# Cross attention: softmax sums inverted in SBUF, turned maxima placed by DMA, values and sums issued apart

## The chip, the cores and the metric

One core of one Trainium2 chip. The metric is the device time of one execution in microseconds. The kernel is a whole decoder layer; the change touches one of its stages.

## The reference

A decoder layer on x (2 batches, 2048 positions, 512 features, float32) does self attention, then cross attention, then a feed-forward part with experts. The change lies in the cross attention: 16 heads of 32 features, 154 keys per batch.

```python
scores = jnp.einsum('bhtd,bhsd->bhts', q, k) * scale
scores = jnp.where(causal_mask[None, None], neg_inf, scores)
scores = jnp.where(key_padding_mask[:, None, None, :], neg_inf, scores)
attn = jax.nn.softmax(scores, axis=-1)
out = jnp.einsum('bhts,bhsd->bhtd', attn, v)
```

Queries beyond position 153 see all keys, so of each batch's four blocks of 512 queries only the first has a causal mask.

## The kernel before

`cross_attention` (from line 1186) works in 32 units: eight blocks of 512 queries (two batches of four) times four groups of four heads. Units 0 to 3 and 16 to 19 are causal. For a unit there are these parts, spread over the units around it:

- `scores(u, s)`, eight slots of two 128-query tiles of one head, queries on partitions, 154 keys along the row (L1325). q and k are stacks of 96 rows (high and low parts), with rows for maxima and padding beneath. Causal units add the mask with a bf16 matmul against an identity (L1328). Slots go to three banks of `ps_s`.
- DVE takes the negated maximum of each slot (`slot_max`, L1404), splits the 16 columns of a unit in a high and a low part (`max_rows` of DVE, L1414 and L1416) in `max_parts`.
- `turn_max(u)` on TensorE (L1338) multiplies `max_parts`, 128 columns of which 8 hold values, with an identity, so that the maxima lie along rows; ACT copies two rows for each of four heads into rows 96 and 97 of `q_stack` (L1460).
- `transposed_scores(u, t)`, eight tiles (four heads, two halves of 77 keys) with keys on partitions, the maxima subtracted by the two added rows (L1350; causal units add a mask, L1353); ACT takes the exponential of each (L1469). These tiles and the turn share the three banks of `ps_st`.
- `weighted_values(u)` (L1364) and `totals(u)`, the sums of the probabilities over keys (L1373), each 16 matmul instructions in the trace, into one bank, `ps_pv` and `ps_d`. ACT copies `ps_pv` to `attn_raw` (L1476).
- DVE inverts the sums in place in PSUM, in four pieces of 128 columns (`invert`, L1422), multiplies (`normalize`, L1429), and SP stores the result (L1290).

The order on each engine is written out by hand. TensorE in unit u issues for t = 0 to 7 a transposed tile of u and a scores slot of u + 2 (called a tile below, together); ahead of t = 3 stand the turn of u + 1, the weighted values and the totals of u - 1. `totals(u)` waits until `normalize(u - 1)` has read `ps_d`. DVE puts the reciprocals between the slots, two pieces behind slots 3 and 4 and two behind slots 0 and 1 of the next unit, and the normalization behind slot 2. ACT follows TensorE's order. `transposed_scores(u, 0)` waits for ACT's copies of the maxima.

SP loads in order: q of unit 0, both stacks of k of batch 0 (that for scores and that for transposed scores), identities, masks, q of unit 1, v, q of units 2 and 3, k of batch 1, and the weights of the next stage (`ahead`, 2.5 MB), which GpSimd splits in two parts (L71, L74). No load among these waits for computed data. Then, per unit, it stores unit u - 2 and loads q of unit u + 4 into the buffer that unit u has left. TensorE starts once all constants and masks are there (`consts_loaded`, 80).

## Time and profile before

| what | us |
|---|---|
| median of three runs | 3406.66 |
| lowest and highest run | 3405.03, 3454.39 |
| the profiled execution, its time | 3420.66 |
| its span, first to last instruction | 3418.9 |
| TensorE busy in the span | 3061.5 |
| DVE busy | 2181.1 |
| ACT busy | 1672.3 |
| GpSimd busy | 1718.2 |
| mean granted clock of TensorE, as a share of 2.4 GHz | 0.925 |
| the cross attention, from its first memset to the last store's landing | about 2433 to 2862 |

The profiled execution is one of its own; its time stands between the runs, and its span is 1.8 us less than its time. Times in the trace count from the span's start. A granted clock of 1.00 is 2.4 GHz and of 0.50 is 1.2 GHz; values between are means over a stretch that has both. Instructions are merged in the timelines when they are alike and adjacent; their ends are modelled for matmuls, so the start of the next is the better mark.

### The profile page before, as it was taken

What the parts mean: (1) busy time and instruction counts of PE and PEld (TensorE: products, weight loads), DVE (VectorE), ACT (ScalarE), POOL (GpSimd) and SP (SyncE); (2) the same over time, 40 slices, a digit from 0 to 9 for tenths busy, and PEclk for the clock granted to TensorE, in tenths of its full rate; (3) what the DMA queues carried; (4) which work ended last, traced back from release to release, by engine and by line L of the source; (5) the groups of instructions that cost most, each with busy time, mean ns of one, the idle gap of its engine ahead of it and who ended that gap; (6) DMA issues with size and microseconds to landing.
All of it is one profiled execution on the core that took longest, in us unless ns stands there. A gap on an engine that the chain in (4) does not pass through costs nothing. (4 is left out here: it accounts for less than half of the span.)

```text
span 3418.9 us, 41782 instructions
## 1 busy us (share of the span) xinstructions
PE 3061.5 (90%) x15214; PEld 1750.2 (51%) x15214; DVE 2181.1 (64%) x3987; ACT 1672.3 (49%) x3029; POOL 1718.2 (50%) x694
## 2 busy tenths in 40 slices
PE   7997999999999999999999997696489986989488
PEld 6875444444444444444444442575345542777433
DVE  4334788788888888888888882463265574566322
ACT  2221466666666666666666665221076672222111
POOL 0001388787888878788888878000210001333255
PEclk9998799999999999999999999798696796999679
DMA  4545545646456464465554443597632232333621
GB/s 173 182 174 171 114 93 107 135 94 151 86 109 135 104 143 99 102 133 108 129 113 96 90 93 65 184 265 169 178 113 86 83 94 106 123 123 116 215 72 35
DMA packets 171357, 424.22 MB, mean 124 GB/s; under 512 B 19105, under 2 KB 40514, under 8 KB 151172
## 3 DMA queue, kind: packets, MB, share of 16 engines
q1 hardware_dynamic: 147038, 276.97, 27.9%
q0 software_dynamic: 24128, 144.75, 20.1%
q8 instruction: 115, 1.88, 0.2%
q14 instruction: 76, 0.62, 0.1%
HBM read 170.20 MB, written 124.58 MB: 86 GB/s over the span
## 5 line engine op out<-in xcount | busy, mean ns | idle before, releaser
L654 DVE TENSOR_REDUCE part_max<-ps_s 128x1 f32<-128x512 f32 x2048 | 1270.3, 679 | 313.2 <-PE ps_s L555 313.2
L751 ACT ACTIVATE probs<-ps_st 128x512 f32<-128x512 f32 x2048 | 1086.4, 600 | 549.3 <-PE ps_st L574 533.9
L513 POOL TENSOR_TENSOR added<-added,probs 128x2048 f32<-128x2048 f32 x256 | 1181.9, 4617 | 93.0 <-ACT probs L751 66.9
L555 PE MATMUL ps_s<-k_stack,q_stack 96*128 96x512 f32 x2048 | 842.1, 427 | 28.3 <-POOL max_parts L503 20.6
L574 PE MATMUL ps_st<-q_stack,k_stack 98*128 98x512 f32 x2048 | 857.7, 424 | 6.6 <-ACT probs L751 5.4
L574 PEld LDWEIGHTS ps_st<-q_stack,k_stack 98*128 98x128 f32 x2048 | 386.9, 190 | 505.6 <-ACT probs L751 362.1
L585 PE MATMUL ps_pv<-probs,v_sb 128*32 128x512 f32 x4096 | 547.2, 606 | 0.0
L555 PEld LDWEIGHTS ps_s<-k_stack,q_stack 96*128 96x128 f32 x2048 | 396.0, 193 | 213.9 <-DVE part_max L654 142.8
L521 POOL DMA_DIRECT2D probs<-probs x128 | 112.7, 880 | 232.7 <-PE ps_pv L585 219.1
L1404 DVE TENSOR_REDUCE xneg_max<-xps_s 128x2 f32<-128x308 f32 x256 | 110.6, 448 | 130.8 <-PE xps_s L1325 82.2
L1654 POOL MEMSET e_bias_rows<- 128x1024 f32 x1 | 1.0, 952 | 354.3 <-POOLq L46 354.3
L1325 PE MATMUL xps_s<-xks_stack,xq_stack 99*128 99x154 f32 (+1 forms) x512 | 130.7, 336 | 49.1 <-DVE xident_r L1436 38.7
L513 POOL TENSOR_TENSOR added<-probs 128x2048 f32<-128x2048 f32 x32 | 146.3, 4570 | 48.7 <-ACT probs L751 48.7
L679 DVE RECIPROCAL ps_d<-ps_d 128x128 f32<-128x128 f32 x128 | 121.0, 949 | 63.2 <-PE ps_d L600 63.2
L585 PEld LDWEIGHTS ps_pv<-probs,v_sb 128*32 128x32 f32 x4096 | 80.8, 108 | 151.8 <-ACT probs L751 122.8
L1325 PEld LDWEIGHTS xps_s<-xks_stack,xq_stack 99*128 99x128 f32 (+1 forms) x512 | 116.4, 234 | 76.8 <-issue 43.4
L1469 ACT ACTIVATE xprobs<-xps_st,xpad_bias 77x512 f32<-77x512 f32 x192 | 119.3, 683 | 69.5 <-PE xps_st L1350 67.1
L1422 DVE RECIPROCAL xps_d<-xps_d 128x128 f32<-128x128 f32 x128 | 120.5, 948 | 19.4 <-PE xps_d L1373 19.4
L1350 PE MATMUL xps_st<-xq_stack,xkt_stack 98*77 98x512 f32 x256 | 122.9, 487 | 1.0 <-ACT xq_stack L1460 0.8
L229 DVE TENSOR_TENSOR qk_l_out<-ps_g,qk_h_out 128x512 fp32r<-128x512 f32 x64 | 43.3, 688 | 125.9 <-ACT qk_h_out L266 125.9
L187 POOL TENSOR_TENSOR rstd<-var_eps,minus_half 128x4 f32<-128x4 f32 x8 | 8.1, 1014 | 224.4 <-DVE var_eps L207 224.4
L1460 ACT ACTIVATE xq_stack<-xps_st 2x512 fp32r<-2x512 f32 x128 | 75.2, 588 | 70.7 <-PE xps_st L1338 69.1
(268 smaller groups left out, 3633.1 us busy)
## 6 DMA issues: line engine op xcount, KB each, us to landing
probs<-probs POOLq DMA_DIRECT2D x128, 1024.0 KB, 7.0
xq_stack<-q_parts SPq DMA_DIRECT2D x64, 384.0 KB, 4.4
q_stack<-q_hi SPq DMA_DIRECT2D x64, 256.0 KB, 6.1
k_stack<-k_hi SPq DMA_DIRECT2D x64, 256.0 KB, 9.0
q_parts<-q_h_out SPq DMA_DIRECT2D x64, 256.0 KB, 4.9
x_in<-in_x_rows SPq DMA_DIRECT2D x8, 1024.0 KB, 7.1
q_hi<-qk_h_out SPq DMA_DIRECT2D x8, 1024.0 KB, 4.3
q_lo<-qk_l_out SPq DMA_DIRECT2D x8, 1024.0 KB, 6.3
```

Of the source, the lines that this page charges most:

```text
L513: pool.tensor_tensor(added[:, w % 2], left, probs[:, k % RING], ALU.add).then_inc(added_up, 1)
L521: pool.dma_start(probs[:, k % RING].rearrange("p j q -> p (j q)"), probs[:, (k - 1) % RING].rearrange("p j q -> p (j q)"), accum_op=ALU.ad ...
L555: pe.matmul(ps_s[:, place % BANKS], q_stack[0:ROWS, w % 4, j, t * P:(t + 1) * P], k_stack[0:ROWS, w // BPB, j, n * BLK:(n + 1) * BLK], sta ...
L574: pe.matmul(ps_st[:, n % BANKS], k_stack[:, w // BPB, j, k * P:(k + 1) * P], q_stack[:, w % 4, j], start=True, stop=True).then_inc(item_do ...
L585: mm = pe.matmul(ps_pv[j * HD:(j + 1) * HD], v_sb[:, w // BPB, k, j * HD:(j + 1) * HD], probs[:, k % RING, j], start=(k == 0), stop=(k == ...
L654: dve.tensor_reduce(part_max[:, s:s + 1], ps_s[:, (w * SLOTS + s) % BANKS], AX.X, ALU.max)\
L679: dve.reciprocal(ps_d[:, cols], ps_d[:, cols]).then_inc(inverted, 1)
L751: act.activation(probs[:, k % RING, j], ps_st[:, n % BANKS], ACT.Exp, scale=SCALE).then_inc(item_used, 1)
L1325: mm = pe.matmul(out, q_stack[0:top, u % BUFS, j, t * P:(t + 1) * P], ks_stack[0:top, batch(u), u % QUADS * HEADS + j], start=True, stop=n ...
L1350: mm = pe.matmul(out, kt_stack[:, batch(u), u % QUADS * HEADS + j, h * KH:(h + 1) * KH], q_stack[0:TOP, u % BUFS, j], start=True, stop=not ...
L1422: dve.reciprocal(ps_d[:, cols], ps_d[:, cols]).then_inc(inverted, 1)
L1469: act.activation(probs[:, u % 2, t % 2, t // 2], ps_st[0:KH, n % BANKS], ACT.Exp, scale=SCALE, **bias)\
```

## The change

1. `totals(u)` is copied by ACT from PSUM to a new tile `sums` in SBUF (`sums_out`); DVE inverts it there in two pieces of 256 columns and the normalization reads it there. `totals(u)` now waits for the copy of u - 1, not for its normalization.
2. `max_parts` has 8 columns per tile, so that the turn writes 8 rows. ACT copies them in one instruction to a new tile `row_parts`, and SP places two rows for each of the four heads in `q_stack` with four DMAs (`rows_into_place`); `transposed_scores(u, 0)` waits for these.
3. The turn stands ahead of t = 2, the weighted values ahead of t = 4, the totals behind t = 7. DVE's first piece stands ahead of slot 4, its second and the normalization at the unit's end, both for unit u - 2. The store is a unit later.
4. The loads are reordered: q of unit 1 ahead of the transposed k, masks last; the rows of unit 0 ahead of v and the q of units 2 and 3, and those of unit 1 ahead of the k of batch 1 and the weights ahead. Waits are split, so that scores start without the transposed k and masks.

```diff
-        BEFORE_TURN = 3
+        BEFORE_TURN = 2
+        BEFORE_VALUES = 4
+        PIECES = 2
...
-        max_parts = sb("xmax_parts", [P, TPB, P], F32R)
+        max_parts = sb("xmax_parts", [P, TPB, 2 * HEADS], F32R)
+        row_parts = sb("xrow_parts", [2 * HEADS, 2, BLK], F32R)
...
+        sums = sb("xsums", [P, 2, BLK])
...
-        k_loaded = [sem(f"xk_loaded{b}") for b in range(B)]
+        ks_loaded, kt_loaded = ([sem(f"x{n}_loaded{b}") for b in range(B)] for n in ("ks", "kt"))
...
+        rows_loaded = [sem(f"xrows_loaded{s}") for s in range(2)]
...
-                def load_k(b):
-                    sp.dma_start(ks_stack[0:ROWS, b].bitcast(F32), xk_parts[:, b]).then_inc(k_loaded[b], 16)
+                def load_scores_k(b):
+                    sp.dma_start(ks_stack[0:ROWS, b].bitcast(F32), xk_parts[:, b]).then_inc(ks_loaded[b], 16)
                     sp.dma_start(ks_stack[TOP:TOP + 1, b].bitcast(F32),
-                                 pad_row[b].unsqueeze(0).unsqueeze(0).to_broadcast([1, H, SC])).then_inc(k_loaded[b], 16)
-                    sp.dma_start(kt_stack[0:ROWS, b].bitcast(F32), xk_parts[:, b]).then_inc(k_loaded[b], 16)
+                                 pad_row[b].unsqueeze(0).unsqueeze(0).to_broadcast([1, H, SC])).then_inc(ks_loaded[b], 16)
+
+                def load_transposed_k(b):
+                    sp.dma_start(kt_stack[0:ROWS, b].bitcast(F32), xk_parts[:, b]).then_inc(kt_loaded[b], 16)
...
                 sp.wait_ge(ones_set, 2)
                 load_q(0)
-                load_k(0)
+                load_scores_k(0)
                 sp.dma_start(ident[:], eye).then_inc(consts_loaded, 16)
                 sp.dma_start(ident_bf[:], eye_bf).then_inc(consts_loaded, 16)
                 sp.dma_start(mq[:].rearrange("p b t k -> p (b t k)"), mask_q).then_inc(consts_loaded, 16)
...
                 sp.wait_ge(ones_set, 4)
-                sp.dma_start(mk[0:KH].rearrange("p b h k -> p (b h k)"), mask_k).then_inc(consts_loaded, 16)
-                sp.dma_start(pad_bias[:], pad_scaled).then_inc(consts_loaded, 16)
                 load_q(1)
+                load_transposed_k(0)
+                sp.dma_start(mk[0:KH].rearrange("p b h k -> p (b h k)"), mask_k).then_inc(masks_loaded, 16)
+                sp.dma_start(pad_bias[:], pad_scaled).then_inc(masks_loaded, 16)
+
+                def rows_into_place(u):
+
+                    sp.wait_ge(item_used, turn_item(u) + 1)
+                    for j in range(HEADS):
+                        sp.dma_start(q_stack[ROWS:TOP, u % BUFS, j].bitcast(F32),
+                                     row_parts[2 * j:2 * j + 2, u % 2].bitcast(F32)).then_inc(rows_loaded[u % 2], 16)
+
+                rows_into_place(0)
                 sp.dma_start(v_sb[:], xv_rows).then_inc(v_loaded, 16)
                 load_q(2)
                 load_q(3)
-                load_k(1)
-                ahead.load(sp)
-                for u in range(UNITS + 2):
-                    if exists(u - 2):
-                        n, g = (u - 2) // QUADS, (u - 2) % QUADS
-                        sp.wait_ge(normalized, u - 1)
-                        sp.dma_start(out_units[n // BPB, n % BPB, g], attn_out[:, u % 2]).then_inc(out_stored[u % 2], 16)
+                for u in range(UNITS + 3):
+                    if exists(u + 1):
+                        rows_into_place(u + 1)
+                    if u == 0:
+                        load_scores_k(1)
+                        load_transposed_k(1)
+                        ahead.load(sp)
+                    if exists(u - 3):
+                        n, g = (u - 3) // QUADS, (u - 3) % QUADS
+                        sp.wait_ge(normalized, u - 2)
+                        sp.dma_start(out_units[n // BPB, n % BPB, g], attn_out[:, (u - 3) % 2])\
+                          .then_inc(out_stored[(u - 3) % 2], 16)
                     if exists(u + BUFS):
                         sp.wait_ge(item_done, item(u, TILES - 1) + 1)
                         load_q(u + BUFS)
...
-                                                   (max_parts[:].bitcast(F32), 0.0), (ones[:], 1.0))):
+                                                   (ones[:], 1.0))):
...
-                        pe.wait_ge(k_loaded[batch(u)], 48)
+                        pe.wait_ge(ks_loaded[batch(u)], 32)
...
-                        mm = pe.matmul(ps_st[:, n % BANKS, t * P:(t + 1) * P], max_parts[:, t], ident_r[:],
+                        mm = pe.matmul(ps_st[0:2 * HEADS, n % BANKS, t * P:(t + 1) * P], max_parts[:, t], ident_r[:],
...
                     if t == 0:
-                        pe.wait_ge(item_used, turn_item(u) + 1)
+                        pe.wait_ge(rows_loaded[u % 2], 64 * (u // 2 + 1))
+                        pe.wait_ge(kt_loaded[batch(u)], 16)
+                        pe.wait_ge(masks_loaded, 32)
...
                 def totals(u):
                     if u:
-                        pe.wait_ge(normalized, u)
+                        pe.wait_ge(sums_done, u)
...
-                pe.wait_ge(ones_set, 6)
-                pe.wait_ge(consts_loaded, 80)
+                pe.wait_ge(ones_set, 5)
+                pe.wait_ge(consts_loaded, 48)
...
                     scores(1, s)
                 for u in range(UNITS + 1):
                     for t in range(TILES):
-                        if t == BEFORE_TURN:
-                            if exists(u + 1):
-                                turn_max(u + 1)
-                            if exists(u - 1):
-                                weighted_values(u - 1)
-                                totals(u - 1)
+                        if t == BEFORE_TURN and exists(u + 1):
+                            turn_max(u + 1)
+                        if t == BEFORE_VALUES and exists(u - 1):
+                            weighted_values(u - 1)
                         if exists(u):
                             transposed_scores(u, t)
                         if exists(u + 2):
                             scores(u + 2, t)
+                    if exists(u - 1):
+                        totals(u - 1)
...
                 def invert(u, q):
-                    cols = slice(q * P, (q + 1) * P)
-                    dve.wait_ge(dens_done, u + 1)
-                    dve.reciprocal(ps_d[:, cols], ps_d[:, cols]).then_inc(inverted, 1)
+                    cols = slice(q * BLK // PIECES, (q + 1) * BLK // PIECES)
+                    dve.wait_ge(sums_done, u + 1)
+                    dve.reciprocal(sums[:, u % 2, cols], sums[:, u % 2, cols]).then_inc(inverted, 1)
 
                 def normalize(u):
                     dve.wait_ge(raw_done, u + 1)
                     if u >= 2:
                         dve.wait_ge(out_stored[u % 2], 16 * (u // 2))
-                    dve.wait_ge(inverted, TPB * (u + 1))
-                    dve.tensor_tensor(attn_out[:, u % 2], ps_d[:], attn_raw[:, u % 2], ALU.mult).then_inc(normalized, 1)
+                    dve.wait_ge(inverted, PIECES * (u + 1))
+                    dve.tensor_tensor(attn_out[:, u % 2], sums[:, u % 2], attn_raw[:, u % 2], ALU.mult).then_inc(normalized, 1)
...
                 for u in range(UNITS + 2):
                     for s in range(SLOTS):
+                        if s == BEFORE_VALUES and exists(u - 2):
+                            invert(u - 2, 0)
                         if exists(u + 2):
                             slot_max(u + 2, s)
-                        if exists(u - 2) and s < 2:
-                            invert(u - 2, s + 2)
-                        if exists(u - 2) and s == 2:
-                            normalize(u - 2)
-                        if exists(u - 1) and 3 <= s < 5:
-                            invert(u - 1, s - 3)
                     if exists(u + 2):
                         max_rows(u + 2)
+                    if exists(u - 2):
+                        invert(u - 2, 1)
+                        normalize(u - 2)
...
                 def max_rows(u):
                     n = turn_item(u)
                     act.wait_ge(item_done, n + 1)
-                    for j in range(HEADS):
-                        mm = act.activation(q_stack[ROWS:TOP, u % BUFS, j], ps_st[j * HD:j * HD + 2, n % BANKS], ACT.Copy)
-                    mm.then_inc(item_used, 1)
+                    if u >= 2:
+                        act.wait_ge(rows_loaded[u % 2], 64 * (u // 2))
+                    act.activation(row_parts[:, u % 2], ps_st[0:2 * HEADS, n % BANKS], ACT.Copy).then_inc(item_used, 1)
...
-                act.wait_ge(ones_set, 6)
-                act.wait_ge(consts_loaded, 80)
+                def sums_out(u):
+                    if u >= 2:
+                        act.wait_ge(normalized, u - 1)
+                    act.wait_ge(dens_done, u + 1)
+                    act.activation(sums[:, u % 2], ps_d[:], ACT.Copy).then_inc(sums_done, 1)
+
                 max_rows(0)
+                act.wait_ge(masks_loaded, 32)
                 for u in range(UNITS + 1):
                     for t in range(TILES):
-                        if t == BEFORE_TURN:
-                            if exists(u + 1):
-                                max_rows(u + 1)
-                            if exists(u - 1):
-                                raw_out(u - 1)
+                        if t == BEFORE_TURN and exists(u + 1):
+                            max_rows(u + 1)
+                        if t == BEFORE_VALUES and exists(u - 1):
+                            raw_out(u - 1)
                         if exists(u):
                             exponentials(u, t)
+                    if exists(u - 1):
+                        sums_out(u - 1)
```

## Rows read from the trace of the kernel before

**Rows 1.** Windows of the cross attention: busy us (instructions) by engine, granted clock, DMA share, GB/s

```profile
2496.00:2514.00 18.00, 16.10 (x71) 8.14 (x71) 10.59 (x16) 7.63 (x14) 11.77 (x5) 0.62 0.21 60
2514.00:2589.00 75.00, 64.77 (x462) 34.91 (x464) 55.76 (x114) 59.31 (x100) 0.00 (x0) 1.00 0.37 109
2589.00:2692.00 103.00, 103.00 (x448) 55.87 (x444) 48.84 (x97) 53.24 (x84) 0.00 (x0) 0.50 0.22 64
2692.00:2822.00 130.00, 114.55 (x819) 62.06 (x817) 94.46 (x193) 99.97 (x169) 0.00 (x0) 1.00 0.35 100
2822.00:2862.00 40.00, 30.57 (x118) 8.36 (x118) 16.82 (x24) 14.53 (x25) 0.00 (x0) 0.53 0.07 27
...
2684.60:2691.20 6.60, 6.60 (x30) 4.48 (x27) 3.43 (x6) 2.38 (x4) 0.00 (x0) 0.50 0.00 0
```

**Rows 2.** Grouped instructions of nine units at clock 1.00, 2726.68 to 2816.88 us

```profile
L1469 ACT ACTIVATE xprobs<-xps_st,xpad_bias 77x512 f32<-77x512 f32 x72 | 43.4, 682 | 19.6 <-PE xps_st L1350 19.6
L1422 DVE RECIPROCAL xps_d<-xps_d 128x128 f32<-128x128 f32 x36 | 34.3, 952 | 0.0
...
L1460 ACT ACTIVATE xq_stack<-xps_st 2x512 fp32r<-2x512 f32 x37 | 21.7, 588 | 0.5
...
L1429 DVE TENSOR_TENSOR xattn_out<-xps_d,xattn_raw 128x512 f32<-128x512 f32 x9 | 6.1, 673 | 0.0
```

**Rows 3.** Waits in the same stretch: total us, times, longest us

```profile
DVE xneg_max L1404 <- PE xps_s L1325: 23.3, 9, 2.6
```

**Rows 4.** Timeline of one unit at clock 1.00: start, us, engine, line, instruction

```profile
2744.10 0.66 PE L1338 MATMUL xps_st<-xident_r,xmax_parts 128*128 128x128 f32 x4
...
2744.69 1.92 PE L1364 MATMUL xps_pv<-xprobs,xv_sb 77*32 77x512 f32 x16
...
2747.46 1.92 PE L1373 MATMUL xps_d<-xprobs,xones 77*32 77x512 f32 x16 [0.85 <-DVE xattn_out L1429]
...
2749.32 0.46 PE L1350 MATMUL xps_st<-xq_stack,xkt_stack 98*77 98x512 f32 x1
...
2749.80 0.40 PE L1350 MATMUL xps_st<-xq_stack,xkt_stack 98*77 98x512 f32 x1
...
2750.22 0.40 PE L1350 MATMUL xps_st<-xq_stack,xkt_stack 98*77 98x512 f32 x1
```

**Rows 5.** Timeline of TensorE around 2612 us, at clock 0.50

```profile
2612.01 0.63 PE L1350 MATMUL xps_st<-xq_stack,xkt_stack 98*77 98x512 f32 x1
...
2612.77 1.03 PE L1338 MATMUL xps_st<-xident_r,xmax_parts 128*128 128x128 f32 x4
2613.74 3.64 PE L1364 MATMUL xps_pv<-xprobs,xv_sb 77*32 77x512 f32 x16
2617.15 3.64 PE L1373 MATMUL xps_d<-xprobs,xones 77*32 77x512 f32 x16
2620.72 0.71 PE L1350 MATMUL xps_st<-xq_stack,xkt_stack 98*77 98x512 f32 x1
```

**Rows 6.** Timeline of TensorE: last tile before unit 2, its first, unit 30's first

```profile
2495.19 0.44 PE L1350 MATMUL xps_st<-xq_stack,xkt_stack 98*77 98x512 f32 x1
...
2496.00 0.43 PE L1350 MATMUL xps_st<-xq_stack,xkt_stack 98*77 98x512 f32 x1
...
2822.19 1.29 PE L1350 MATMUL xps_st<-xq_stack,xkt_stack 98*77 98x512 f32 x3
```

**Rows 7.** First load; window of loads; landings of pad rows (L1267), then of output stores (L1290)

```profile
2444.04 0.79 SPq L1262 DMA_DIRECT2D xq_stack<-q_parts  x2
...
2460.00:2470.00 10.00, 7.16 (x39) 7.03 (x39) 4.51 (x12) 0.00 (x0) 0.00 (x0) 0.50 1.03 255
...
DMA to landing us min/median/max: 9.1/15.9/22.6
...
DMA to landing us min/median/max: 2.3/2.3/4.6
```

**Rows 8.** Timeline near 2497 us: DVE's cast of the maxima

```profile
2496.75 1.36 DVE L1414 CAST xmax_parts<-xneg_max 128x16 fp32r<-128x16 f32 x1
```

More of the change, by code:

```diff
@@ L1225, in cross_attention @@
                                            for n, (_, high, _) in enumerate(weights_ahead)])
-        k_loaded = [sem(f"xk_loaded{b}") for b in range(B)]
+        ks_loaded, kt_loaded = ([sem(f"x{n}_loaded{b}") for b in range(B)] for n in ("ks", "kt"))
         v_loaded = sem("xv_loaded")
         q_loaded = [sem(f"xq_loaded{s}") for s in range(BUFS)]
-        consts_loaded, ones_set, ident_ready = sem("xconsts_loaded"), sem("xones_set"), sem("xident_ready")
+        consts_loaded, masks_loaded = sem("xconsts_loaded"), sem("xmasks_loaded")
+        ones_set, ident_ready = sem("xones_set"), sem("xident_ready")
         scores_done, max_done = sem("xscores_done"), sem("xmax_done")
@@ L1232, in cross_attention @@
         item_done, item_used = sem("xitem_done"), sem("xitem_used")
+        rows_loaded = [sem(f"xrows_loaded{s}") for s in range(2)]
         pv_done, dens_done = sem("xpv_done"), sem("xdens_done")
-        raw_done, inverted, normalized = sem("xraw_done"), sem("xinverted"), sem("xnormalized")
+        raw_done, sums_done = sem("xraw_done"), sem("xsums_done")
+        inverted, normalized = sem("xinverted"), sem("xnormalized")
         out_stored = [sem(f"xout_stored{s}") for s in range(2)]
@@ L1304, in _ @@
                     pool.memset(tile, value).then_inc(ones_set, 1)
-                pool.wait_ge(ones_set, 6)
+                pool.wait_ge(ones_set, 5)
                 for step in range(ahead.STEPS):
@@ L1433, in slots @@
                         slot_max(u, s)
-                dve.wait_ge(consts_loaded, 80)
+                dve.wait_ge(consts_loaded, 48)
                 dve.tensor_copy(ident_r[:], ident[:]).then_inc(ident_ready, 1)
-                dve.wait_ge(ones_set, 6)
+                dve.wait_ge(ones_set, 5)
                 for u in range(2):
```

## The prediction

> **What bounds the kernel now.** I read the stage's windows first. The reader is to see one stage at two speeds: from 2589 to 2692 us TensorE is busy for all of the 103 us and its granted clock is 0.50, the 1.2 GHz level; from 2692 to 2822 us it is at 1.00, 2.4 GHz, and busy for only 114.55 of 130 us [rows 1]. At the low level TensorE itself is the bound. At the high level something else is, and the grouped instructions of nine units there say what: 72 exponentials are nine times eight, so a unit takes 90.2 / 9 = 10.02 us, in which ACT holds four copies of two rows at 588 ns each beside eight exponentials, and DVE four reciprocals at 952 ns beside eight maxima [rows 2]. The waits show the loop that sets the 10.02: DVE is idle 2.6 us per unit for scores [rows 3]. The timeline tells why: weighted values start at 2744.69, the sums could follow at once, but wait 0.85 us for the normalization, because that reads the sums in PSUM; then the sums, 1.86 us to the next transposed scores, stand between the normalization and DVE's next scores [rows 4]. So DVE works, then TensorE works, and each waits for the other.
>
> At 1.2 GHz a tile (transposed scores and scores) takes 2612.77 - 2612.01 = 0.76 us, the turn 0.97, the weighted values 3.41, the sums 3.57: 8 x 0.76 + 7.95 = 14.0 us, with nothing idle [rows 5].
>
> **The change part by part.**
>
> *Sums copied to SBUF.* It adds one ACT copy of 128x512, which no row of mine shows by itself; bounds are the 588 ns of a 2x512 copy and the 682 ns of an exponential with bias [rows 2]. I take 0.6. It removes the wait of the sums for the normalization (0.85 us, and the 2.6 us of DVE behind it), as PSUM is free again after that copy.
>
> *Reciprocals, two of 256 columns for four of 128.* Bounds: 0.95 us (width costs nothing) and 1.90 us (twice the row) for one [rows 2]. I take 1.8, near the upper end, as an iterated division should go by column. DVE's work was 94.46 us in 130, which is 7.3 us in a unit of 10.02 [rows 1]; it becomes about 7.2.
>
> *Turned maxima in eight rows.* Three of four ACT copies go, 3 x 0.588 = 1.76 us of ACT a unit, 0.6 comes back for the sums: ACT, a near bound, is left with some 6.9 us. The turn itself writes 8 rows in place of 128; its 0.59 us (2744.10 to 2744.69) lies between 0.3 and 0.6, I take 0.5 [rows 4]. Its matmul needs no more DVE work than now.
>
> *Four row DMAs per unit on SP's queue,* behind the turn's copy. The next transposed scores now wait for them. One output store lands in 2.3 us [rows 7], issued in some 0.35; four issues and a landing are 1.4 + 2.3 = 3.7 us after the copy. The turn is at tile 2, six tiles, the weighted values and the sums before the next unit: 6 x 0.42 at least + 3.6 = 6.1 us of cover less 1.5 for copy and handoff, so 4.6 against 3.7: hidden by about a microsecond. Bounds: 0, and, if each took the 9.1 us that a small transfer took behind large ones, 4.5 us a unit [rows 7]. In the steady state nothing large is ahead of them: the q loads are issued at a unit's end, some 3.5 us earlier. I take 0. SP's queue is in order: the rows are issued before the output store, both before the q load of the same turn, which waits last; nothing else of SP's is urgent.
>
> *Weighted values at tile 4, sums at the unit's end.* No work changes. DVE's first reciprocal (1.8) now lies beside the weighted values (1.8), its second, with the normalization (0.67), beside the sums (1.86), and three score banks bridge the rest. By hand for a unit at 2.4 GHz: TensorE 8 x 0.43 + 0.5 + 1.8 + 1.85 = 7.6; DVE 7.2 plus about 0.5 of handoffs. I take 7.75 (low 7.3, ACT's and DVE's sum; high 9.0, if half of the old handoff is left).
>
> *The beginning,* an estimate from one rate. Scores can start earlier, as they no longer wait for the transposed k and masks. But SP now sits at unit 0's turn before it issues v and q of units 2 and 3, and at unit 1's before the second k and the weights ahead, 4.3 MB. Before, these were issued without such waits. SP's first load goes out at 2444.04, and the DMA moves 255 GB/s [rows 7]. What the first scores need is 2.2 MB, so they begin near 2456; eight slots and the turn later, near 2465, ACT releases the rows of unit 0; after them v and one q, 1.4 MB, land at about 2474, where unit 0 starts (before at 2475.4). Its turn comes some 5 us later, so the 4.3 MB and the next q, 5.2 MB or 20 us, flow from about 2483.5. The rows of unit 2 are issued behind them. The row of the small pad transfer shows what that does: 9.6 KB took 9.1 and 22.6 us to land behind large loads [rows 7]. So unit 2 starts near 2503.7, not at 2496.00 [rows 6]: plus 7.7 us, and TensorE is idle for about 9 us ahead of it. Bounds: 0 and 12.
>
> *Sum.* From unit 2 to unit 30 the kernel took 2822.19 - 2496.00 = 326.2 us for 28 units [rows 6]. After: 20 units without causal work x 7.75 = 155; 14 and 15 (causal scores only), tile between 0.42 and 0.81, taken 0.55: 8.7 each; 16 and 17, 0.81 a tile [rows 6]: 8 x 0.81 + 4.2 = 10.7 each; 18, 19 and 3 (causal transposed scores only), tile 0.63: 9.2 each; unit 2, partly at 1.2 GHz: 14. In all 155 + 17.4 + 21.4 + 27.6 + 14 = 235.4: minus 90.8. The start adds 7.7. The tail of 40 us at clock 0.53 [rows 1] loses about 2.5 us of idleness. Net minus 85.6 on the profiled execution's 3420.7: 3335. Its own time is 14 us above the median of the runs, 3406.7, and the low stretch (103 us) may be shorter in those, of which little remains here; other stages may account for some of it. I take 2 off: 3333 us.
>
> **The clock, and a page.** Of the 90.8 us, 103 x (1 - 10.02 / 14.0) = 29 come from the low stretch alone, which is assumed at 2.4 GHz. Before TensorE's clock fell there, it had run turn, weighted values and the wait for DVE as in every unit [rows 4]; before it rose again it had been busy for the whole 6.6 us up to 2691.2, in tiles with causal mask matmuls [rows 1]. Tiles without them, eight between sums and turn, did not bring it back. The new order leaves no pause at 2.4 GHz, so I expect no fall; but after the pause at unit 2 it needs a rise, and its runs of tiles are cut in two.
>
> The Trainium skill, TensorE: Matmul & The Clock Gate, section "Why this matters for your kernels", says that TensorE that is kept continuously busy gets the full clock. The trace disagrees: 103 us without idleness at 0.50 [rows 1]. By the page the clock would be back within unit 2 and the result some 5 us lower; by the row it may not rise for ten units, which is the first rival below.
>
> A second page speaks against the move to SBUF: SBUF — State Buffer, section "SBUF: two separate sides", says that a VectorE instruction with two SBUF inputs and a GpSimd instruction block one another. The normalization becomes such an instruction. The trace agrees in kind: a cast of 16 columns took 1.36 us while GpSimd split weights [rows 8], and GpSimd is busy 11.77 of those 18 us [rows 1]. It has no work later in this stage, so by the page it is at most a few microseconds, once, beside unit 2.
>
> **The rivals.**
>
> *The clock stays low after the start (chance 0.18; the other side).* The mechanism: TensorE's pause before unit 2 drops it to 1.2 GHz; units 2 and 3 have causal mask matmuls in their tiles but now in two runs of four with weighted values or sums between, and if they don't lift it, ten units without causal work don't either, as those of the low stretch did not. Price: 10 x (14.0 - 7.75) = 62, units 2 and 3 +11, 14 and 15 +15, half of 16 +5: 93 us, so 3426, slower than 3406.7. It decides at unit 3's end. For it: the 103 us. Against: a pause at 2498 us also lowered the clock (0.62 over 2496 to 2514) and causal units brought it back by 2514 [rows 1].
>
> *Rows come late (0.10).* If four landings follow one another or queue behind the q load, each unit waits 1 to 1.5 us for them: 24 x 1.2 = 29: 3362. For: the 22.6 us row. Against: the 2.3 us row.
>
> *The start costs nothing (0.10).* If the loads drain sooner, or small transfers pass, unit 2 starts at 2496 and the clock holds: 3333 - 8 (the start) - 7 (the low part of units 2 and 3) = 3318.
>
> *Forecast (0.62),* own range 3305 to 3360: 7.4 to 8.6 a unit is -7 to +17 on 20 units, the start -5 to +5.
>
> **How the numbers follow.** The range 3302 to 3428 takes in the forecast, the cheap start, the late rows and half of the low clock. About 2% (68 us) is what a measurement of this kernel tells from no change, so faster means below 3338.5. Of the forecast 0.6 lies there (0.37), of the cheap start all (0.10), of the late rows little (0.01): faster 0.48, same 0.47, slower 0.05 (the clock low also past unit 20, another 60 us or more).
>
> **What would show it.** Units at 2.4 GHz 7.5 to 8 us apart; 256-column reciprocals near 1.8 us and starting beside weighted values and sums; no wait of sums for the normalization; DVE's wait for scores under 0.5 us a unit; row DMAs landing in 2 to 3 us with transposed scores not waiting for them after unit 2; a pause of 5 to 12 us before unit 2. A unit above 9 us at clock 1.00 refutes the handoff argument; a stretch of clock 0.50 from unit 2 to unit 16 is the first rival.

## The result, and the profile after

The changed kernel takes 3331.23 us (median of 3329.57, 3330.77, 3331.69 and 3414.33), against 3426.44 for the kernel before in the same rounds (3405.03 to 3454.39): ratio 0.9731, interval 0.967 to 0.9791. The forecast was 3333. The ratio leaves out the fourth run, which had a mean granted clock of 0.917 where the profiled one had 0.946; it lies near the 3426 at which the first rival was priced, and is told of below.

The windows of the cross attention, in the columns of [rows 1], cut where the clock changed:

```profile
2481.00:2498.00 17.00, 14.41 (x114) 8.67 (x112) 7.00 (x18) 9.34 (x16) 0.00 (x0) 1.00 0.89 255
2498.00:2508.30 10.30, 4.81 (x19) 3.35 (x19) 1.36 (x3) 2.36 (x4) 6.75 (x3) 0.50 0.67 177
2508.30:2530.00 21.70, 20.36 (x151) 10.56 (x150) 19.15 (x29) 13.04 (x23) 9.67 (x4) 1.00 0.32 88
2530.00:2600.00 70.00, 69.09 (x512) 37.55 (x508) 65.18 (x112) 52.72 (x93) 0.00 (x0) 1.00 0.45 128
2600.00:2700.00 100.00, 99.43 (x761) 54.84 (x758) 87.07 (x144) 68.54 (x122) 0.00 (x0) 1.00 0.41 120
2700.00:2760.00 60.00, 57.45 (x416) 29.28 (x419) 53.38 (x84) 45.86 (x82) 0.00 (x0) 1.00 0.35 100
```

One dip to 0.50, then 1.00 to the end. The 103 us stretch of [rows 1] is gone, and TensorE is busy for 99% where it was busy for 88%. The grouped instructions of 2530 to 2600 us answer to [rows 2]:

```profile
L1494 ACT ACTIVATE xprobs<-xps_st,xpad_bias 77x512 f32<-77x512 f32 x68 | 41.4, 676 | 0.0
L1448 DVE RECIPROCAL xsums<-xsums 128x256 f32<-128x256 f32 x18 | 31.4, 1743 | 0.0
...
L1455 DVE TENSOR_TENSOR xattn_out<-xsums,xattn_raw 128x512 f32<-128x512 f32 x8 | 5.5, 692 | 1.1
L1501 ACT ACTIVATE xattn_raw<-xps_pv 128x512 f32<-128x512 f32 x9 | 5.4, 598 | 9.7 <-PE xps_pv L1390 9.7
```

68 exponentials in 70 us are 8.5 units of 8.2 us; ACT's copies of the weighted values, one a unit, stand 8.27 us apart, where they stood 10.02. The reciprocal of 256 columns takes 1743 ns. The waits of the same stretch:

```profile
PEld xps_st L1376 <- ACT xprobs L1494: 10.0, 17, 0.8
ACT xattn_raw L1501 <- PE xps_pv L1390: 9.7, 9, 1.1
ACT xsums L1507 <- PE xps_d L1399: 7.7, 8, 1.0
...
DVE xneg_max L1430 <- PE xps_s L1349: 2.2, 9, 0.3
```

DVE's wait for scores was 2.6 us a unit in [rows 3] and is 0.3. No wait of the sums for the normalization is left in this stretch. What is late now is in the first line: twice a unit the weight load of a transposed tile waits for an exponential to free its PSUM bank. TensorE's timeline of one unit shows what that costs:

```profile
2558.96 0.46 PE L1376 MATMUL xps_st<-xq_stack,xkt_stack 98*77 98x512 f32 x1
...
2559.44 0.40 PE L1376 MATMUL xps_st<-xq_stack,xkt_stack 98*77 98x512 f32 x1
...
2559.86 0.41 PE L1362 MATMUL xps_st<-xident_r,xmax_parts 128*8 128x128 f32 x4
2560.38 0.46 PE L1376 MATMUL xps_st<-xq_stack,xkt_stack 98*77 98x512 f32 x1
...
2560.95 0.46 PE L1376 MATMUL xps_st<-xq_stack,xkt_stack 98*77 98x512 f32 x1
...
2561.53 1.92 PE L1390 MATMUL xps_pv<-xprobs,xv_sb 77*32 77x512 f32 x16
2563.38 0.46 PE L1376 MATMUL xps_st<-xq_stack,xkt_stack 98*77 98x512 f32 x1
...
2565.37 1.07 PE L1399 MATMUL xps_d<-xprobs,xones 77*32 77x512 f32 x8
```

From start to start: tiles 0.48 and 0.42, turn 0.52, tiles 0.57 and 0.58, values 1.85, and the other four tiles 1.99 (2563.38 to 2565.37); the sums, 2557.10 to 2558.96, took 1.86. Together 8.27 us: in each group of four tiles the last two follow one another at 0.5 to 0.6 us, nearer to ACT's 0.68 for an exponential than to TensorE's 0.43.

The beginning, TensorE and SyncE before unit 2:

```profile
2491.11 2.43 SPq L1296 DMA_DIRECT2D xq_stack<-xrow_parts  x4
...
2503.49 0.71 PE L1376 MATMUL xps_st<-xq_stack,xkt_stack 98*77 98x512 f32 x1 [8.07 <-DMA xq_stack<-xrow_parts]
```

The first line is SyncE issuing the four row DMAs of unit 2, behind 4.3 MB of loads; TensorE waits 8.07 us for them, the only wait of the stage for row DMAs. Each of the 128 row DMAs took 0.56 to 0.70 us to issue.

### The profile page after: what moved, and what is told of

The parts are those of the page before. It is cut to its first block and busy times, and to the rows that moved or that the text cites. A ratio compares the mean times of both kernels' runs of the same rounds, so it can differ in the third digit from the quotient of the medians.

```text
span 3327.8 us, 41873 instructions
## 1 busy us (share of the span) xinstructions
PE 2984.6 (90%) x15214; PEld 1715.5 (52%) x15214; DVE 2191.5 (66%) x3923; ACT 1620.7 (49%) x2965; POOL 1718.3 (52%) x693
## 5 line engine op out<-in xcount | busy, mean ns | idle before, releaser
L1349 PE MATMUL xps_s<-xks_stack,xq_stack 99*128 99x154 f32 (+1 forms) x512 | 113.5, 300 | 42.0 <-DVE xident_r L1462 32.5
L1349 PEld LDWEIGHTS xps_s<-xks_stack,xq_stack 99*128 99x128 f32 (+1 forms) x512 | 104.4, 205 | 59.8 <-issue 43.9
L1376 PE MATMUL xps_st<-xq_stack,xkt_stack 98*77 98x512 f32 x256 | 111.4, 440 | 12.7 <-DMA xq_stack<-xrow_parts 8.1
L1448 DVE RECIPROCAL xsums<-xsums 128x256 f32<-128x256 f32 x64 | 111.0, 1740 | 6.1 <-ACT xsums L1507 6.1
L908 POOL TENSOR_TENSOR c_rstd<-c_var_eps,c_minus_half 128x4 f32<-128x4 f32 x8 | 8.1, 1009 | 195.5 <-DVE c_var_eps L941 195.5
```

Source lines behind the costliest of these rows:

```text
L1349: mm = pe.matmul(out, q_stack[0:top, u % BUFS, j, t * P:(t + 1) * P], ks_stack[0:top, batch(u), u % QUADS * HEADS + j], start=True, stop=n ...
L1376: mm = pe.matmul(out, kt_stack[:, batch(u), u % QUADS * HEADS + j, h * KH:(h + 1) * KH], q_stack[0:TOP, u % BUFS, j], start=True, stop=not ...
```

## The experiments

The "unit" below is the distance of ACT's copies of the weighted values in units without causal work.

**Sums left in PSUM** (`e1_psum`).

```diff
-                        pe.wait_ge(sums_done, u)
+                        pe.wait_ge(normalized, u)
...
-                    dve.reciprocal(sums[:, u % 2, cols], sums[:, u % 2, cols]).then_inc(inverted, 1)
+                    dve.reciprocal(ps_d[:, cols], ps_d[:, cols]).then_inc(inverted, 1)
...
-                    if exists(u - 1):
-                        sums_out(u - 1)
```

The normalization reads `ps_d` again.

> The changed kernel with the sums left in PSUM: no ACT copy of them, both 256-column reciprocals and the normalization work on PSUM, and the sums of a unit wait for the normalization of the one before. Order, row DMAs and loads as changed. Theory (the handoff over PSUM is what cost 2 us a unit): the sums at a unit's end wait for a reciprocal and the normalization, about 2.5 us, and a unit without causal work goes from 8.27 back to 10.0 to 10.8 us at clock 1.00; total 3375 to 3430, the upper half if the clock falls as well. Rival (the new order alone, with fewer copies on ACT, gives the gain): under 9 us a unit and under 3345.

Measured 3596.5 us (3592.9 to 3601), ratio 1.0497 (1.0418 to 1.0577). Its waits of 2600 to 2700 us, and the end of one unit:

```profile
DVE xneg_max L1430 <- PE xps_s L1349: 51.0, 47, 4.7
...
PEld xps_d L1399 <- DVE xattn_out L1455: 18.6, 5, 3.7
```

```profile
2612.20 3.64 PE L1399 MATMUL xps_d<-xprobs,xones 77*32 77x512 f32 x16 [3.51 <-DVE xattn_out L1455]
...
2616.86 0.48 DVE L1430 TENSOR_REDUCE xneg_max<-xps_s 128x2 f32<-128x308 f32 x1 [4.72 <-PE xps_s L1349]
```

The wait returns, as expected, but at 3.51 us a unit, and the clock is at 0.50 for the whole of that window. A unit takes 17.7 us: the 14.2 of 1.2 GHz plus the wait. The time is 166 us above the top of what was expected, because I had priced the units at clock 1.00. The clock fell at 2543 us, behind the first such wait at 1.00 (3.48 us, up to 2542.26), and was 0.50 from 2550 to 2760. So the copy to SBUF is what makes the rest of the new order work, and the first such wait at 1.00 was followed by the loss of the clock as well. That the later waits kept the clock down is not shown: `e6_b_sums` and `e3_late` have long stretches at 0.50 without any idle.

**That copy alone, in the kernel before** (`e6_b_sums`), with its four pieces:

```diff
-                        pe.wait_ge(normalized, u)
+                        pe.wait_ge(sums_done, u)
...
                                 raw_out(u - 1)
+                                sums_out(u - 1)
```

> The kernel before with one part of the change: ACT copies the sums to SBUF, right behind the weighted values' copy, and DVE inverts them there in four pieces. Theory (the copy pays only with the new order and the freed ACT): the 0.85 us wait of TensorE goes, but ACT has 8.7 us of work in a unit and the copy stands ahead of five exponentials: 9.3 to 9.9 us a unit, total 3385 to 3420. Rival: 8.3 us and under 3350.

Measured 3432.81 us (3404 to 3453, ten runs), ratio 1.004 (0.9998 to 1.0081). The unit at clock 1.00 is 8.96 us, a little quicker than expected; the total is not, by these windows:

```profile
2532.00:2678.00 146.00, 146.00 (x630) 79.06 (x630) 74.17 (x151) 88.25 (x140) 0.00 (x0) 0.50 0.25 73
2700.00:2760.00 60.00, 57.82 (x420) 32.09 (x419) 47.37 (x97) 54.15 (x93) 0.00 (x0) 1.00 0.40 120
```

The 1.06 us a unit were won and given back by a longer low stretch (146 us, where [rows 1] had 103) and a second one from 2764. The copy is needed, and not enough. No long idle stood ahead of either fall. Ahead of the first one:

```profile
2500.00:2532.00 32.00, 30.82 (x220) 18.29 (x223) 26.57 (x56) 29.01 (x50) 3.10 (x2) 1.00 0.41 124
...
2530.10 0.45 PE L1327 MATMUL xps_s<-xks_stack,xq_stack 99*128 99x154 f32 x2 [0.51 <-DVE xneg_max L1406]
```

The longest wait of TensorE there is this one of 0.51 us, which comes once in most units of this kernel, and the same wait stands at 2762.20 ahead of the second fall. Why the clock fell at these units, and in the kernel before at 2589 us, is open.

**Turn, values and sums together ahead of tile 3, sums in SBUF** (`e5_together`).

```diff
-        BEFORE_TURN = 2
-        BEFORE_VALUES = 4
+        BEFORE_TURN = 3
+        BEFORE_VALUES = 3
...
                             weighted_values(u - 1)
+                            totals(u - 1)
...
                             raw_out(u - 1)
+                            sums_out(u - 1)
```

The two calls at the unit's end are gone.

> The changed kernel with turn, weighted values and sums together ahead of tile 3, as before (raw and sums copies by ACT there too; DVE's first reciprocal ahead of slot 3). Sums in SBUF, row DMAs and loads as changed. Theory (the two stretches of 1.8 us must be apart, since three score banks hold DVE's work for one of them only): DVE waits some 1.5 us for scores, 9.3 to 10.2 us a unit at clock 1.00, total 3352 to 3400. Rival (the copy to SBUF alone gives the gain): 8.1 to 8.5 us a unit, 3331.

Measured 3333.8 us (3329.8 to 3341.9), ratio 0.9763 (0.9701 to 0.9824), unit 8.28, and from 2570 to 2640 us TensorE busy for 69.76 of 70 at clock 1.00. The theory is refuted and the rival holds: the order of values and sums gives nothing that this can measure. With the copy and without four row copies, both orders run alike.

**Rows by four ACT copies in place of four DMAs** (`e2_rows_act`); the turn writes 128 rows again and `rows_into_place` is gone.

```diff
-                    act.activation(row_parts[:, u % 2], ps_st[0:2 * HEADS, n % BANKS], ACT.Copy).then_inc(item_used, 1)
+                    for j in range(HEADS):
+                        mm = act.activation(q_stack[ROWS:TOP, u % BUFS, j], ps_st[j * HD:j * HD + 2, n % BANKS], ACT.Copy)
+                    mm.then_inc(item_used, 1)
```

> The changed kernel with the maxima turned into 128 rows and copied by ACT in four pieces straight into the q stack, as before; no row DMAs, so SP's loads wait for nothing at the start. Theory: ACT gets 1.75 us more in a unit, which its waits of 1.9 us in 8.27 do not all cover: 8.6 to 9.2 us a unit, 20 units give plus 7 to 19; the pause of 8 us ahead of unit 2 is gone (minus 8 to 15); total 3322 to 3342. Rival (the row DMAs are what carries the gain): 10 us a unit, 3360 or more. Rival (the row DMAs cost what they save): 8.27 a unit and 3318.

Four runs: 3352.2, 3353.9, 3425.9 and 3429.8 us, the last two at mean clock 0.916 and 0.915 against 0.94. In the profiled run (3353.9) the unit is 9.17 us at clock 1.00, so the DMAs are worth 0.9 us a unit in the steady state. The pause before unit 2 is absent: the values' copies around it stand 14.70 us apart (2490.43 and 2505.13), 20.40 in the changed kernel, so the DMAs cost 5.7 us there. The unit is as expected; the total is 10 to 12 us above the top of what was expected in the two runs at 0.94, and over 80 in the others. Those two show that a run some 75 us longer at a lower mean clock comes without the 8 us pause too; they have no profile.

**The burst of loads moved from unit 0 to unit 4** (`e3_late`).

```diff
-                    if u == 0:
+                    if u == 4:
                         load_scores_k(1)
                         load_transposed_k(1)
                         ahead.load(sp)
```

> The changed kernel with the k of batch 1 and the weights ahead loaded at unit 4 and not at unit 0. Theory (these 4.3 MB in front of the rows of unit 2 make the pause of 8 us and the drop of the clock): no pause ahead of unit 2, units unchanged at 8.27 us; total 3314 to 3322, and no run near 3414 in three rounds, as nothing lowers the clock before ten units that cannot lift it. Rival (the pause is hidden, or the rows come late by themselves): 3328 to 3334; rival for the one run at 3414 (its source lies elsewhere): such a run comes here too.

Measured 3392.16 us (3390.4 to 3400.2, ten runs), ratio 0.9938 (0.9911 to 0.9965): 61 us slower than the changed kernel. Its timeline at unit 6 and a window behind it:

```profile
2546.27 0.71 PE L1376 MATMUL xps_st<-xq_stack,xkt_stack 98*77 98x512 f32 x1 [10.29 <-DMA xq_stack<-xrow_parts]
```

```profile
2550.00:2698.00 148.00, 148.00 (x640) 75.22 (x640) 82.27 (x129) 70.49 (x110) 8.07 (x4) 0.50 0.25 73
```

The pause went with the burst, which shows its cause. The expected 3314 to 3322 was missed by 70 us: I had not seen that the burst would hold the rows of unit 6 in place of those of unit 2. There no unit with causal tiles follows soon, and the clock stays at 0.50 with TensorE busy for all of these 148 us. This is the first rival's mechanism. The profiled run shows it; all ten runs have a mean clock of 0.921 to 0.924, so it came in each.

**ACT's sums copy behind two exponentials of the next unit** (`e4_sums_later`).

```diff
+                        if t == BEFORE_TURN and exists(u - 2):
+                            sums_out(u - 2)
...
-                    if exists(u - 1):
-                        sums_out(u - 1)
```

> The changed kernel with ACT's copy of the sums moved behind two exponentials and the copy of the maxima of the next unit. Theory (8.27 and not 7.75 us, because the copy of the sums stands ahead of the exponential that frees the bank for the tile behind the turn): 7.8 to 8.0 us a unit, total 3321 to 3328. Rival (DVE's two reciprocals of 1.74 us set 8.27): 8.2 to 8.3 us and no change.

Measured 3328.12 us (3326.8 to 3336.5), ratio 0.9715 (0.9643 to 0.9788); the unit 8.18 us, 0.09 less and not the 7.8 to 8.0 of the theory. TensorE has no idle time left (60.00 of 60 us busy). I read DVE, idle for 1.3 us in 60 by its waits, as the bound. That reading was tested next. The start of this run shows something else:

```profile
2508.00:2528.00 20.00, 19.79 (x79) 10.60 (x80) 9.01 (x15) 6.95 (x13) 13.82 (x5) 0.50 0.15 43
```

The pause before unit 2 is nearly that of the changed kernel (7.29 us for 8.07), but TensorE, busy again from 2506.25, stays at 0.50 for 22 us, into the middle of unit 3, the last causal one of the first batch; in the changed kernel it was 5 us.

**1.6 us of DVE work a unit taken away** (`e9_short`, `e10_short_sums`): the second reciprocal of a unit inverts 16 columns and leaves 240 uninverted, in the changed kernel and in the last one.

```diff
-                    cols = slice(q * BLK // PIECES, (q + 1) * BLK // PIECES)
+                    cols = slice(q * BLK // PIECES, (q + 1) * BLK // PIECES) if q == 0 else slice(BLK // 2, BLK // 2 + 16)
```

> The changed kernel with the second reciprocal of a unit cut from 256 columns to 16 (half of the sums then stays uninverted, which the output shows): about 1.6 us of VectorE work less a unit, nothing else changed. A unit took 8.27 us, with VectorE 7.7 us of it busy. Theory A (the ring of TensorE and ScalarE through the turned exponentials, with ScalarE's copy of the sums ahead of the next unit's first exponential, sets the 8.27 us, and VectorE only follows): a unit stays at 8.1 to 8.27 us, and TensorE stays busy all but 0.1 us of it. Theory B (VectorE's 7.7 us with its handoffs set it): a unit of 7.5 to 7.7 us, TensorE's own work being 7.4 to 7.6 at clock 1.00, and over the stage some 14 us less.

> The same cut with ScalarE's copy of the sums moved behind the next unit's second exponential, where a unit took 8.18 us and VectorE was idle for only 0.16 us of it. Theory (in that kernel VectorE sets the unit, by 8.0 us of busy time and handoffs): with 1.6 us of its work gone TensorE's own work is left, a unit of 7.5 to 7.8 us, 12 to 20 us less over the stage than the 8.18 us unit makes. Rival (TensorE sets 8.18 as well, its busy time being counted too short by the model of matmul ends): a unit stays at 8.1 to 8.2 us and the time within 3 us of 3328.

One run each: 3332.4 and 3328.6 us, units of 8.27 and 8.14. Windows 2540 to 2600 us of the first, and its DVE wait:

```profile
2540.00:2600.00 60.00, 59.21 (x442) 31.83 (x431) 47.19 (x96) 44.85 (x81) 0.00 (x0) 1.00 0.45 135
```

```profile
DVE xneg_max L1430 <- PE xps_s L1349: 9.9, 22, 0.5
```

DVE's work fell from 56.00 us in the changed kernel to 47.19 in this window and the unit did not move: DVE only waits more. Theory A holds in the changed kernel, and in the other my DVE theory falls, the rival holding at 8.14 against 8.18. What is left to set the unit is TensorE and ACT's exponentials through the PSUM banks. Which of those two, and whether a fourth bank would give the rest, was not tried.

**The burst spread: k loads at units 2 and 3, the next stage's three weights one at a time at units 15 to 17** (`e7_spread`), and the same with the later sums copy (`e8_spread_sums`).

```diff
-                    if u == 0:
+                    if u == 2:
                         load_scores_k(1)
+                    if u == 3:
                         load_transposed_k(1)
-                        ahead.load(sp)
+                    if 15 <= u < 15 + len(ahead.weights):
+                        source, raw, _, _ = ahead.weights[u - 15]
+                        sp.dma_start(raw, source).then_inc(ahead.loaded, 16)
```

> The changed kernel with the k of batch 1 loaded at units 2 and 3 and the three weights ahead at units 15, 16 and 17, one load of about 1 MB at a time behind the rows. Theory (a burst of 4.3 MB ahead of the rows makes the pause, and a pause lets the clock fall, for ten units where they have no causal work): no pause of over 2 us behind unit 0, clock 1.00 from about 2487 us to the end of the stage, 8.27 us a unit; total 3314 to 3323, and none of the runs of five rounds above 3350. Rival (the one run at 3414 has a source elsewhere): again a run some 80 us above the others. Rival (any single load of 1 MB delays the rows past 8.27 us): pauses of 1 to 3 us in units 3, 4 and 16 to 18.

> The spread loads together with ACT's copy of the sums behind the copy of the maxima. Theory: both gains add, 8.18 us a unit as measured with the copy moved alone: 2 us below the run with spread loads, 3311 to 3321, and the interval of its ratio to the kernel before below 0.975. Rival: GpSimd's work at units 17 to 19 meets DVE's and costs back 2 us or more.

Measured 3329.59 (3326.3 to 3337.6; ratio 0.9749) and 3325.74 us (3321.9 to 3330.0 and one of 3399.51; ratio 0.9735, 0.9683 to 0.9788). Both are above what was expected (3314 to 3323 and 3311 to 3321). The pause before unit 2 is gone, the clock is 1.00 from 2482 us; but GpSimd now splits the weights beside busy units, all three in one stretch, since it waits for the last of them (`pool.wait_ge(self.loaded, 16 * len(self.weights))`). The second kernel there:

```profile
2636.36 4.64 POOL L74 TENSOR_TENSOR xwo_w_l<-xahead_raw,xwo_w_h 128x2048 fp32r<-128x2048 f32 x1
2640.84 2.00 POOL L71 CAST xwo_w_h<-xahead_raw 128x2048 fp32r<-128x2048 f32 x1
...
2643.82 0.71 PE L1352 MATMUL xps_s<-xks_stack,xq_stack 99*128 99x154 f32 x2 [5.51 <-DVE xneg_max L1433]
```

```profile
2636.24 1.74 DVE L1451 RECIPROCAL xsums<-xsums 128x256 f32<-128x256 f32 x1
2638.11 5.27 DVE L1458 TENSOR_TENSOR xattn_out<-xsums,xattn_raw 128x512 f32<-128x512 f32 x1
```

The normalization, 0.69 us elsewhere, takes 5.27 and ends at 2643.38, after GpSimd's cast. TensorE is idle for 5.51 us, and the clock goes to 0.50 for 10 us. In the first kernel a normalization took 3.17 us there and TensorE was idle for 3.43. The rival written down for the second run holds. The run at 3399.51 has no profile, and its cause is open.

**The weights at units 28 to 30** (`e11_tail_sums`) **and at 4, 6 and 8** (`e12_early_sums`), both with the k loads at 2 and 3 and the later sums copy.

```diff
-                    if 15 <= u < 15 + len(ahead.weights):
-                        source, raw, _, _ = ahead.weights[u - 15]
+                    if u in (28, 29, 30):
+                        source, raw, _, _ = ahead.weights[(28, 29, 30).index(u)]
```

> The changed kernel with the sums copy moved as before, the two k loads at units 2 and 3, and the three weight loads of the next stage at units 28, 29 and 30, where VectorE has its last reductions behind it, in place of all five at unit 0. Theory (the 4.3 MB burst makes the 8 us pause of unit 2, and the 5.5 us stall of the kernel that loaded the weights at units 15 to 17 was GpSimd's splitting of them meeting VectorE): neither the pause nor a stall, the clock at 1.00 from about 2482 to the end, units of 8.18 us, and 3328 less 12 to 15 us: 3312 to 3318. Rival 1 (the split at the end holds the next stage's first work or the last reciprocals up): 3318 to 3328. Rival 2 (the clock falls anyway at some later unit, since another short idle comes): 3330 or more, ten or more units of 14 us.

> As the kernel with the weights at the end, but the three weight loads at units 4, 6 and 8, so that GpSimd splits them one at a time inside units without causal work, where VectorE has 0.16 us to spare of 8.18. Theory (GpSimd's 16.5 us of splitting slow VectorE's copies and reciprocals through SBUF, wherever it stands): TensorE waits 1 us or more for the slot maxima at one or more of the three places, 4 to 12 us in all, 3318 to 3330, and more if the clock falls over one such wait (at 6 us a unit). Rival (it was only the causal units, where TensorE does most, that could not take the meeting): no wait above 1 us and the time of the kernel with the weights at the end, within 3 us.

With the weights at the end: 3317.48 us (3315.3 to 3323.9, six runs), ratio 0.9677 (0.9634 to 0.972), the fastest of this study. Two of its windows:

```profile
2500.00:2560.00 60.00, 60.00 (x441) 32.87 (x439) 55.09 (x94) 44.25 (x79) 0.00 (x0) 1.00 0.57 153
2560.00:2720.00 160.00, 159.74 (x1204) 87.07 (x1203) 143.97 (x240) 113.51 (x203) 0.00 (x0) 1.00 0.44 125
```

TensorE has no pause and no stall: the theory. GpSimd does meet DVE at the end (one normalization took 4.46 us, at 2749.06), where no scores are left to wait for it. With the weights early: 3356.36 us (3344.2 to 3368.8), ratio 0.9787 (0.9738 to 0.9836). TensorE waited 1.48 and 1.38 us for the slot maxima, less in all than the 4 to 12 us expected, for GpSimd again split everything in one stretch from 2554 us and not at three places. But the clock fell over the first of them: 0.50 from 2558 to 2647 us. A cast of that stretch:

```profile
2564.61 4.37 DVE L1443 CAST xmax_parts<-xneg_max 128x16 fp32r<-128x16 f32 x1
```

"And more if the clock falls over one such wait" applied: 38.9 us above the same kernel with the weights at the end.

## Why the prediction was right

3333 was forecast, 3331.2 measured. The handoff's part is shown: with the sums in PSUM it returns (e1), and the copy alone takes 1.06 us off a unit (e6). That the gain hangs on the clock is shown too: with a long stretch at 0.50 the kernel gains 0.6% and not 2.7 (e3). What made the clock fall in the kernel before is not shown; the forecast's "no pause, so I expect no fall" came true, but in e6 it fell twice with no wait above 0.51 us. In the profiled executions the time comes out so, before and after: unit 2 to unit 30 326.2 and 2749.66 - 2503.49 = 246.2 us, minus 80.0; unit 2 starts at 2503.49 and not 2496.00, plus 7.5; from unit 30 to the next stage's first instruction 2862.28 - 2822.19 = 40.1 and 2777.45 - 2749.66 = 27.8, minus 12.3; all behind it minus 6.3, to which the forecast gave at most its 2. Sum minus 91.1, the difference of the spans. The 6.3 us lie in other stages, which were not changed: the clock was 0.81 over 3280 to 3320 us before and 0.98 over the corresponding stretch after (3196 to 3236).

*The unit* was the mis-sized term: 7.75 forecast, 8.27 measured, 20 x 0.52 = 10.4 us of the 10.8 by which units 2 to 30 missed. "TensorE 8 x 0.43 + 0.5 + 1.8 + 1.85 = 7.6" took every tile at the pace of a tile that waits for nothing. In the trace a run of four tiles takes about 2.0 us without the turn, not 1.7, and I read this off the wait for exponentials of 0.68 us, which free only three banks (`BANKS`). I had weighed ACT by its sum (6.9 us a unit; the rows give 99.97 / 130 x 10.02 - 1.76 + 0.6 = 6.5, and 52.72 / 70 x 8.27 = 6.2 was measured), which hid that the exponentials come in bursts, with ACT idle 1.0 us ahead of each PSUM copy. DVE's sum was also low (7.2; it is 65.18 / 70 x 8.27 = 7.7), but e9 shows that this cost nothing.

*The tail* missed the other way by 9.8 us: I had it at half clock as before, and with no fall ahead of it the clock stayed at 1.00 to 2771 us. The two errors cancel by luck, and the 6.3 us behind the stage come on top; 3333 is nearer than its steps deserve.

*The beginning* was right in place and size (2503.7 forecast, 2503.49 measured; first scores 2454.48 for 2456; TensorE idle 8.07 us for 9), and e3, e7 and e11 show its cause, though they moved the loads together with GpSimd's work. Some of it is luck: this execution issued its first load at 2441.65, 2.4 us earlier than the one before, so from there unit 2 came 2.2 us later than forecast. The clock's return is luck as well: 5 us after the pause here, 7 in e9, but 17 in e5 and 22 in e4 and e10, where the pause is much the same.

*Prices:* reciprocal 1.8 forecast, 1.74 measured; sums copy 0.6, 0.598; turn 0.5, 0.52; units 14 and 15 8.7, 8.98; 16 and 17 10.7, 10.74. Row DMAs were hidden in steady state as forecast, though each issue took 0.57 us and not 0.35: 2.4 + 2.3 = 4.7 us, with the landing still that of a store, as the trace has none of theirs, against the 4.6 of cover that I had. By these numbers the slower tiles, which lengthened the cover, kept the second rival away: the rows' copy of the unit shown ends at 2561.36 and the next unit starts at 2565.37 + 1.86 = 2567.23, 5.9 us later.

*The parts.* I gave the values and sums apart a share in bridging DVE's work; e5 shows none. Of the 1.75 us that a unit lost, the copy is worth 1.06 (e6: 8.96), what e5 has beside it (row DMAs, two-piece reciprocals, the loads' order) 0.68 (8.28), and the order of values and sums 0.01.

*The rivals.* The clock low after the start was priced at 3426: one run of four of the changed kernel took 3414.33 at mean clock 0.917. No profile of that run exists, so its cause is argued only. For it: e3, where such a pause meets units without causal work, shows the mechanism in full, and in e4 and e10 the clock came back only in unit 3. Against: e2, without that pause, had two such runs in four. There TensorE was idle for 0.4 us a unit (76.31 of 80 us busy), in the changed kernel for 0.1, so a fall inside the steady units is a cause that was not tested. The cheap start (3318) is reached by the kernel that has the weights at the end (e11): 3317.5, with 2 to 3 us of the distance to 3331 from the sums copy (20 x 0.09 us by e4's units, 3.1 by its median).

*The pages.* On the clock, TensorE was never idle for 148 us at 0.50 in e3 and for 146 in e6. The Trainium skill, TensorE: Matmul & The Clock Gate, "Why this matters for your kernels", says that continuous work gets the full clock; here the measurement decides against it. Ahead of unit 2 the changed kernel's trace looks as by the page (back after 5 us), and e4's does not (22 us). On SBUF, in the changed kernel a normalization beside GpSimd took at most 1.05 us and a cast of 16 columns 1.80, once each, and TensorE waited 1.23 us for the maxima behind them. The Trainium skill, SBUF — State Buffer, "SBUF: two separate sides", says that whichever starts first holds the shared port for its whole instruction; the 5.27 us normalization agrees in kind: it started inside one GpSimd instruction and ended only after the next, the cast. I had called the risk "a few microseconds, once, beside unit 2", true of this change and false as soon as the loads move.

## What to carry to other kernels

When two engines alternate through one PSUM tile, copying it out breaks the loop for the price of one copy, but the gain is only kept if the clock is up: look at the granted clock of each stretch first, and at every idle of TensorE ahead of units that don't lift it. Here 1.48 us stood ahead of one fall (e12) and no more than 0.51 ahead of another (e6). Size a loop with few PSUM banks by the pace of whoever frees them inside each burst, not by sums over a unit. Before moving a load, ask what small transfers queue behind it and which engine its landing starts: here the same three loads cost 39 us more at units 4 to 8 than at the end.

## What the runs showed of the hardware

- TensorE was continuously busy at 1.2 GHz for 146 and 148 us (e6, e3), mostly in units without causal matmuls. After a pause of 7 to 9 us before a causal unit the clock was back within 5 us in the changed kernel (2503.49 to 2508.3), 7 in e9, 17 in e5, 22 in e4 and e10.
- A TensorE wait as short as 1.48 us, after 70 us with hardly a gap, was followed by 89 us at 0.50 (e12). In e6 the clock fell to 0.50 at 2532 and 2764 us with no wait above 0.51 us ahead.
- A DVE instruction with two inputs in SBUF, begun inside a GpSimd instruction, ended only after the next one (0.69 us became 5.27, e8); so did a cast of 16 columns (0.18 to 4.37, e12). Reciprocals with one SBUF input kept their 1.74 us beside it.
- The reciprocal goes by column in PSUM and SBUF alike: for 128 columns 952 ns in PSUM [rows 2] and 939 in SBUF (e6), for 256 columns 1757 in PSUM (e1) and 1743 in SBUF.
- Four 4 KB DMAs behind 4.3 MB on one queue held TensorE for 8 to 10 us (8.07 in the changed kernel, 10.29 in e3), and each took SyncE 0.57 us to issue.
